# A windowed attention and MLP block on one core: a new order of the stages on every engine, PSUM banks dealt anew, and the first MLP layer in three f16 passes

## The chip, the core and the metric

The kernel runs on one core of one Trainium2 chip. A core has TensorE (PE, matmuls and their weight loads), VectorE (DVE), ScalarE (ACT), GpSimd (POOL) and SyncE (SP, which issues DMAs); each has its own queue of instructions, done in order, and they meet through semaphores. Engines read and write SBUF; matmuls write PSUM, which VectorE and ScalarE read. The metric is the device time of one execution in microseconds.

## What is computed

For 32 images of 96 channels and 56x56 pixels: layer norm over channels, attention with 12 heads of 8 channels inside windows of 7x7 pixels with a bias table, a projection and a residual sum, a 3x3 depthwise convolution with batch norm, and an MLP of 96 -> 384 -> 96 with a residual sum.

```python
xn = _layernorm(xw, ln_g, ln_b)
qkv = (xn @ qkv_w.T + qkv_b).reshape(Bw, N, 3, HEADS, HEAD_DIM)
...
attn = jnp.einsum('bhnd,bhmd->bhnm', q * SCALE, k)
attn = attn + bias.transpose(2, 0, 1)[None]
attn = jax.nn.softmax(attn, axis=-1)
out = jnp.einsum('bhnm,bhmd->bhnd', attn, v)
return out @ proj_w.T + proj_b
...
seq = shortcut + out
conv = lax.conv_general_dilated(x_local, conv_w, (1, 1), ((1, 1), (1, 1)), feature_group_count=DIM)
bn = (conv - bn_mean) * scale + bn_b
h = jax.nn.gelu(seq2 @ w1.T + b1, approximate=False)
seq = seq2 + (h @ w2.T + b2)
```

Inputs, weights and output are f32.

## The kernel before

A **chunk** is seven image rows, that is eight windows of 49 pixels or 392 columns (`CT`); there are 256 chunks, eight to an image. The program is a software pipeline: step n starts chunk n and carries older chunks further, and every engine's queue holds 264 steps, unrolled, with no branch in them. `real(st, lag)` drops what lies outside the 256 chunks. A chunk goes through these stages, with the step's lag in brackets.

- Layer norm (0): `centred` (TensorE, f32, into `d_ps`), the square (ScalarE), `variance` (TensorE, f32, into `a_ps`), logarithm and exponential for the reciprocal root (ScalarE), the product `xn` (VectorE), its f16 upper part `xh` (ScalarE) and lower part `xl` (GpSimd).
- Queries and keys (1): `three` f16 passes each, 392 columns, into `d_ps` and `b_ps`; each result is again split into an upper (ScalarE) and a lower part (VectorE), and SP sends six terms by DMA into `q_all` and `k_all` (`term`, counted by `exp_in`).
- Values (2): twelve f16 matmuls of 96 columns into `b_ps`, copied by ScalarE (`v32` for the even window of a pair) and VectorE (for the odd one).
- Maxima (2): four groups `max_scores` of 24 small matmuls (64 columns of weights, 49 moving) into `sm_ps`, each followed by VectorE's `maxima`; the row maxima are transposed on TensorE (`maxima_rows`), copied by VectorE (`mxt_out`) and sent by DMA into a row of `q_all`.
- Scores (3, the last group at 4): four groups `exp_scores` of 24 into `st_ps`, each followed by ScalarE's exp into `p32`; then four groups `values_times_p` of 12 f32 matmuls into `o_ps`, copied by ScalarE in halves (`outputs`) and sent by GpSimd's DMAs into `ox`.
- Sums' reciprocals (ScalarE) and `normalise` (VectorE), `projection` (TensorE, f32, four pieces, into `b_ps`), and the residual sum into `ximg` (VectorE, `sum_done`), all at 5.
- Convolution (6 and 7): the first tap on GpSimd, `tap` 1 to 8 on VectorE, each adding to `s2`.
- MLP (7 and 8): three `hidden` matmuls (f32, 96 to 128, one for each block of 128) into `a_ps`, `d_ps`, `b_ps`, a gelu each on ScalarE, three `second` matmuls (f32) into `a_ps`, the sum `y` on VectorE and the store. Gelu needs another activation table than exp and logarithm: two table loads a step.

Each engine's order is written out by hand in its `step`. `st_ps` and `sm_ps` have two PSUM banks each; `o_ps`, `a_ps`, `b_ps` and `d_ps` have one each and are shared by the stages above, so a stage also waits until the bank's last reader is done. On TensorE a step ends with `values_times_p(st, 3, 0)`, a wait for the fourth maximum, `values_times_p(st, 3, 1)`, `maxima_rows` and two `hidden`; the third stands at the start of the next step, followed by the first `max_scores`.

## Time and profile before

| | us |
|---|---|
| median of 3 runs | 3758.8 |
| lowest and highest run | 3752.88, 3760.82 |
| the profiled execution | 3757.64 |
| its span, from the first to the last instruction | 3755.8 |
| TensorE busy in the span | 3535.0 |
| ScalarE busy | 3101.7 |
| VectorE busy | 2937.8 |
| GpSimd busy | 1133.5 |

The granted clock of TensorE was 0.996 of full over the span. Busy times of TensorE include matmul ends that are modelled, so distances from one start to the next say more of its pace. Group rows give a count, the busy time and the mean of one; a bracket or a last column names what the engine waited for just before.

### The profile page before, as it was taken

What the parts mean: (1) busy time and instruction counts of PE and PEld (TensorE: products, weight loads), DVE (VectorE), ACT (ScalarE), POOL (GpSimd) and SP (SyncE); (2) the same over time, 40 slices, a digit from 0 to 9 for tenths busy, and PEclk for the clock granted to TensorE, in tenths of its full rate; (3) what the DMA queues carried; (4) which work ended last, traced back from release to release, by engine and by line L of the source; (5) the groups of instructions that cost most, each with busy time, mean ns of one, the idle gap of its engine ahead of it and who ended that gap; (6) DMA issues with size and microseconds to landing.
All of it is one profiled execution on the core that took longest, in us unless ns stands there. A gap on an engine that the chain in (4) does not pass through costs nothing.

```text
span 3755.8 us, 189287 instructions
## 1 busy us (share of the span) xinstructions
PE 3535.0 (94%) x83724; PEld 2303.3 (61%) x83724; DVE 2937.8 (78%) x5155; ACT 3101.7 (83%) x5123; POOL 1133.5 (30%) x1550
## 2 busy tenths in 40 slices
PE   4999999999999999999999999999999999999998
PEld 2666666666666666666666666666666666666664
DVE  4778787877878778787877878787787878778786
ACT  2788888888888888888888888888888888888886
POOL 2232332323233232333233233232323323232332
PEclk9999999999999999999999999999999999999999
DMA  1232332323233232322323233232323223232321
GB/s 46 82 91 85 89 89 84 91 84 91 85 88 90 84 91 84 91 87 87 88 86 91 85 90 90 84 91 84 91 85 89 88 85 92 83 91 84 90 89 47
DMA packets 269476, 321.37 MB, mean 86 GB/s; under 512 B 55124, under 2 KB 252181, under 8 KB 268663
## 3 DMA queue, kind: packets, MB, share of 16 engines
q1 hardware_dynamic: 235894, 232.12, 21.6%
q0 software_dynamic: 32768, 77.14, 6.2%
q8 instruction: 665, 10.90, 1.3%
q14 instruction: 149, 1.21, 0.1%
HBM read 39.35 MB, written 38.54 MB: 21 GB/s over the span
## 4 chain that ended last, share of the span: by engine, by line
PE 76%; ACT 12%; DVE 7%; issue 4%; SPq 1%; DMA 0%; POOL 0%; POOLq 0%; DVEq 0%; ACTq 0%
PE a_ps L438 13%; PE sm_ps L322 10%; PE o_ps L339 8%; PE a_ps L357 6%; PE a_ps L430 6%; DVE mx L673 5%; PE st_ps L307 5%; PE d_ps L349 5%; PE b_ps L430 4%; PE d_ps L430 4%; ACT sq L561 4%; PE b_ps L280 4%; ACT sq L563 4%; ACT sq L557 3%; PE b_ps L282 2%
## 5 line engine op out<-in xcount | busy, mean ns | idle before, releaser
L695 DVE SCALAR_TENSOR_TENSOR s<-ximg,cols,s 96x392 f32<-96x392 f32 x2048 | 1260.0, 615 | 20.8 <-POOL s L597 2.9
L673 DVE TENSOR_REDUCE mx<-sm_ps 128x12 f16<-128x588 f32 x1024 | 780.9, 763 | 435.4 <-PE sm_ps L322 435.4
L597 POOL TENSOR_TENSOR s<-ximg,cols 96x392 f32<-96x392 f32 x256 | 215.6, 842 | 2384.7 <-DVE y L726 2384.7
L499 ACT ACTIVATE p<-st_ps 128x588 f32<-128x588 f32 x1024 | 669.5, 654 | 130.7 <-PE st_ps L307 126.6
L322 PEld LDWEIGHTS sm_ps<-k_all,q_all 127*64 127x64 f16 x24576 | 472.5, 113 | 315.6 <-issue 210.5
L438 PE MATMUL a_ps<-g,w_s 128*96 128x392 f32 x1536 | 602.2, 501 | 0.0
L604 POOL DMA_DIRECT2D ox<-o_sb x1024 | 580.8, 570 | 47.9 <-issue 31.8
L322 PE MATMUL sm_ps<-k_all,q_all 127*64 127x49 f16 x24576 | 580.5, 192 | 7.9 <-DMA q_all<-ql 6.4
L307 PEld LDWEIGHTS st_ps<-q_all,k_all 128*64 128x64 f16 x24576 | 476.1, 113 | 151.8 <-issue 147.9
L307 PE MATMUL st_ps<-q_all,k_all 128*64 128x49 f16 x24576 | 562.3, 191 | 0.0
L339 PE MATMUL o_ps<-p,v 128*32 128x49 f32 x24576 | 428.1, 211 | 131.0 <-DVE mx L673 129.5
L339 PEld LDWEIGHTS o_ps<-p,v 128*32 128x32 f32 x24576 | 322.5, 110 | 324.6 <-DVE mx L673 164.6
L592 POOL TENSOR_TENSOR xl<-xn,xh 96x392 f16<-96x392 f32 x256 | 330.9, 1293 | 172.6 <-ACT xh L567 172.5
L542 ACT ACT_TABLE_LOAD x256 | 328.4, 1283 | 4.5
L536 ACT ACT_TABLE_LOAD x256 | 328.4, 1283 | 4.5
L737 DVE TENSOR_TENSOR xn<-d_ps,sq 96x392 f32<-96x392 f32 x256 | 143.8, 562 | 238.3 <-ACT sq L563 238.3
L438 PEld LDWEIGHTS a_ps<-g,w_s 128*96 128x96 f32 x1536 | 230.9, 164 | 105.2 <-issue 89.6
L567 ACT ACTIVATE xh<-xn 96x392 f16<-96x392 f32 x256 | 138.2, 540 | 160.8 <-DVE xn L737 160.8
L357 PE MATMUL a_ps<-sq,avg 96*96 96x392 f32 x512 | 233.0, 537 | 24.3 <-ACT sq L557 1.8
L557 ACT ACTIVATE sq<-d_ps 96x392 f32<-96x392 f32 x256 | 126.1, 492 | 151.3 <-PE d_ps L349 151.3
L519 ACT ACTIVATE o_sb<-o_ps 128x294 f32<-128x294 f32 x512 | 213.1, 416 | 43.3 <-PE o_ps L339 43.3
L430 PE MATMUL a_ps<-s,w_s 96*128 96x392 f32 x512 | 237.7, 546 | 6.9 <-DVE s L695 6.9
(98 smaller groups left out, 5539.7 us busy)
## 6 DMA issues: line engine op xcount, KB each, us to landing
ox<-o_sb POOLq DMA_DIRECT2D x1024, 73.5 KB, 2.6
k_all<-kh SPq DMA_DIRECT2D x512, 96.0 KB
q_all<-qh SPq DMA_DIRECT2D x512, 96.0 KB
x_sb<-in_x SPq DMA_DIRECT2D x256, 147.0 KB, 2.4
out<-y SPq DMA_DIRECT2D x256, 147.0 KB, 2.9
k_all<-kl SPq DMA_DIRECT2D x256, 96.0 KB
q_all<-ql SPq DMA_DIRECT2D x256, 96.0 KB
q_all<-mxt SPq DMA_DIRECT2D x256, 12.0 KB, 2.0
```

Of the source, the lines that this page charges most:

```text
L307: last = mm(st_ps[64 * w:64 * w + 64, h // HH, c0:c0 + TOK], k_all[:, r, h, n:n + WP], q_all[:, r, h, n:n + TOK], start=True, stop=True)
L322: last = mm(sm_ps[64 * w:64 * w + 64, h // HH, c0:c0 + TOK], q_all[0:MAXROW, r, h, n:n + WP], k_all[0:MAXROW, r, h, n:n + TOK], start=True ...
L339: last = mm(o_ps[32 * c4:32 * c4 + 32, at:at + TOK], v32[:, r, h, q, :], p32[:, q, h, :], start=True, stop=True)
L357: mm(a_ps[0:C, 0:CT], avg[:, :], sq[:, :], start=True, stop=True).then_inc(var_done, 1)
L430: mm(t[:, 0:CT], w1_s[:, k * 128:(k + 1) * 128], s2[0:C, (st[1] - lag) % 2, :], start=True, stop=True)\
L438: last = mm(a_ps[0:C, 0:CT], w2_s[:, k, :], g[:, k, :], start=k == 0, stop=k == NB - 1)
L499: af(p32[:, q, :, :].rearrange("p (b h) n -> p b h n", b=2), st_ps[:, :, 0:HALF].rearrange("p b (h n) -> p b h n", n=TOK), ACT.Exp).then_i ...
L536: af(g[:, k, :], (a_ps, d_ps, b_ps)[k][:, 0:CT], ACT.Gelu, bias=b1_c[:, k:k + 1]).then_inc(g_done, 1)
L592: tt(xl[0:C, r, :, 0:TOK], xn[:, :, :], xh[0:C, r, :, 0:TOK], ALU.subtract).then_inc(xl_done, 1)
L604: nc.gpsimd.dma_start(ox[:, r4, x4, :], o_sb[x4::4, r4, :, :]).then_inc(o_in[r4], 16)
L673: v.tensor_reduce(mx[:, (st[1] - lag) % 2, :, p].rearrange("p (b h) -> p b h", b=2), sm_ps[:, :, 0:HALF].rearrange("p b (h n) -> p b h n", ...
L695: v.scalar_tensor_tensor(acc, image_rows(st, lag, k // 3, k % 3), cw_c[:, k:k + 1], acc, ALU.mult, ALU.add)\
```

## The change

**Order and lags.** All engines get a new order of stages, and each stage names its chunk as `s - lag`; a wait counts chunks, with a semaphore for each of the four parts of a stage. The last `exp_scores` keeps its chunk but moves to the end of a step, and the first `max_scores` moves from lag 2 to lag 1 at the step's very end. `maxima_rows` stands behind the three `hidden`, and `mxt_out`'s copy is the first thing in VectorE's next step. VectorE takes the fourth maximum ahead of the normalisation, and taps 1 and 2 after the image sum. ScalarE does its three gelus between two table loads at the start of a step. SP issues three terms of one chunk, then an input load, the maxima row, and three terms of the next chunk with a store among them; the program has 266 steps.

**Banks.** `centred`, the third `hidden` and all `second` use `b_ps`; variance, queries, projection and one `hidden` use `a_ps`; keys, values and one `hidden` use `d_ps`. `free` waits for a bank's last real reader.

**First MLP layer.** Its input is split into f16 parts by two new GpSimd instructions (`image_high`, `image_low`), its weights, times 256, at setup; each of the three blocks is three f16 passes in place of one f32 matmul.

**Small changes.** Score matmuls load 49 columns of weights instead of 64, so they write 49 of 64 PSUM rows (the rest is set to zero once). The values are copied by one VectorE instruction, which writes two neighbouring words per value with a column of factors that is zero for the other window; ScalarE's copy goes. The setup has two instructions more for the weights, two for the zeros, one load, and the first input loads come behind it.

```diff
-STEPS = CHUNKS + 8
-IMAGE = C * SIDE * SIDE
+STEPS = CHUNKS + 10
...
+        w1_h, w1_l = sb("w1_h", [C, HID], F16), sb("w1_l", [C, HID], F16)
+        sh, sl = sb("sh", [C, CT], F16), sb("sl", [C, CT], F16)
...
+        def free(eng, *users):
+            for s, c in users:
+                if real(c):
+                    eng.wait_ge(s, c + 1)
+                    return
...
+            for s in range(STEPS):
+                term(q_all, 0, qh, qh_done, s - 3)
+                term(q_all, 2, ql, ql_done, s - 3)
+                term(k_all, 2, kh, kh_done, s - 3)
+                load(s)
+                maximum_row(s - 4)
+                first_term(q_all, 1, qh, qh_done, s - 2)
+                term(k_all, 1, kl, kl_done, s - 2)
+                store(s - 10)
+                term(k_all, 0, kh, kh_done, s - 2)
...
+                    free(pe, (mxt_out, c-1), (max_done[3], c-1), (max_done[2], c-1), (max_done[1], c-1), (max_done[0], c-1))
...
+                        last = mm(sm_ps[64 * w:64 * w + TOK, h // HH, c0:c0 + TOK], q_all[0:MAXROW, r, h, n:n + TOK],
                                   k_all[0:MAXROW, r, h, n:n + TOK], start=True, stop=True)
...
+            def hidden(c, k):
+                if not real(c):
+                    return
+                if k == 1:
+                    wait(pe, sl_done, c)
                 if k == 0:
-                    wait(pe, tap_done, st, lag, 8)
-                    if real(st, 0):
-                        wait(pe, lnv_done, st, 0)
-                    else:
-                        wait(pe, y_done, st, 8)
+                    free(pe, (sum_done, c+2), (lnv_done, c+7), (ql_done, c+6), (g_done[0], c-1))
                 elif k == 1:
-                    if real(st, 0):
-                        wait(pe, xn_done, st, 0)
-                    elif real(st, 1):
-                        wait(pe, ql_done, st, 1)
-                    else:
-                        wait(pe, g_done, st, 8, NB, 2)
-                elif real(st, 6):
-                    wait(pe, sum_done, st, 6)
-                t = (a_ps, d_ps, b_ps)[k]
-                mm(t[:, 0:CT], w1_s[:, k * 128:(k + 1) * 128], s2[0:C, (st[1] - lag) % 2, :], start=True, stop=True)\
-                    .then_inc(hid_done, 1)
...
+                    free(pe, (v32_done, c+5), (kl_done, c+6), (g_done[1], c-1))
+                elif k == 2:
+                    free(pe, (xn_done, c+7), (y_done, c-1), (g_done[2], c-1))
+                wide_three(hidden_ps[k][:, 0:CT], w1_h[:, k * 128:(k + 1) * 128], w1_l[:, k * 128:(k + 1) * 128], sh[:, :], sl[:, :]).then_inc(hid_done[k], 1)
+            def second(c, k):
+                if not real(c):
+                    return
+                wait(pe, g_done[k], c)
+                if k == 1:
+                    free(pe, (g_done[2], c+0), (xn_done, c+7), (y_done, c-1))
+                wide(b_ps[0:C, 0:CT], w2_s[:, k, :], g[:, k, :], start=k == 1, stop=k == 0).then_inc(s_done[k], 1)
...
+            for s in range(STEPS):
+                keys(s - 1)
...
+                max_scores(s - 1, 0)
...
+                af(g[:, k, :], {0: a_ps, 1: d_ps, 2: b_ps}[k][:, 0:CT], ACT.Gelu, bias=b1_c[:, k:k + 1], scale=1 / UP).then_inc(g_done[k], 1)
...
+            for s in range(STEPS):
+                act.preload_act_table_set("gelu_and_others")
+                gelu(s - 8, 1)
+                gelu(s - 8, 2)
+                gelu(s - 8, 0)
...
...
+                pool.sem_inc(turn, 1)
+                nc.gpsimd.tensor_copy(sh[:, :], s2[0:C, c % 2, :]).then_inc(sh_done, 1)
+            def image_low(c):
+                if not real(c):
+                    return
+                wait(pool, sh_done, c)
+                tt(sl[:, :], s2[0:C, c % 2, :], sh[:, :], ALU.subtract).then_inc(sl_done, 1)
+            for s in range(STEPS):
+                first_tap(s - 6)
+                to_channels(s - 4)
+                image_high(s - 7)
+                image_low(s - 7)
+                input_low(s)
...
+                wait(dve, v_done, c)
+                wait(dve, pv_done[2], c - 2)
+                v.tensor_tensor(v32[:, c % 2, :, :, :].rearrange("p h n (d x) -> p (h n d) x", x=4)[:, :, 0:2],
+                                d_ps[:, 0:NP * C].unsqueeze(2).broadcast_to([128, NP * C, 2]),
+                                half_c[:, :].unsqueeze(1).broadcast_to([128, NP * C, 2]), ALU.mult).then_inc(v32_done, 1)
...
+            for s in range(STEPS):
+                maxima_out(s - 3)
...
+                tap(s - 6, 2)
...
+    half = np.zeros((128, 2), np.float32)
+    for w in range(2):
+        half[64 * w:64 * w + TOK, w] = 1 / UP
```

On TensorE, from the wait for the fourth maximum to the next step's first maxima group (`o_ps` is the values' product, `sm_ps<-eye_h,mx` the transpose, `a_ps`, `d_ps`, `b_ps<-s,w_s` the first layer). Before:

```order
L339 MATMUL o_ps<-p,v 32x49 [waits p_done,max_done]
L339 MATMUL o_ps<-p,v 32x49 x11
L446 MATMUL sm_ps<-eye_h,mx 48x128
L430 MATMUL a_ps<-s,w_s 128x392 [waits lnv_done,tap_done]
L430 MATMUL d_ps<-s,w_s 128x392 [waits xn_done]
L430 MATMUL b_ps<-s,w_s 128x392 [waits sum_done]
L322 MATMUL sm_ps<-k_all,q_all 64x49 [waits max_done,mxt_out,exp_in1]
L322 MATMUL sm_ps<-k_all,q_all 64x49 x23
```

After, from the last block of the first layer on (`w_h`, `w_l` and `sh`, `sl` are the f16 parts; projection and the other two blocks stand in front of it):

```order
L256 MATMUL a_ps<-sh,w_h 128x392 [waits sum_done]
L257 MATMUL a_ps<-sl,w_h 128x392
L258 MATMUL a_ps<-sh,w_l 128x392
L319 MATMUL sm_ps<-eye_h,mx 48x128 [waits max_done3]
L289 MATMUL st_ps<-q_all,k_all 49x49 [waits p_done2]
L289 MATMUL st_ps<-q_all,k_all 49x49 x23
L310 MATMUL sm_ps<-k_all,q_all 49x49 [waits mxt_out,exp_in1]
L310 MATMUL sm_ps<-k_all,q_all 49x49 x23
```

The transpose with its wait went behind the first layer and behind both value groups, an exp group came between it and the maxima group, and that group, which waits for `mxt_out` and the DMA terms, is now of the chunk that was begun one step ago, directly ahead of the keys.

On VectorE, around the normalisation (`xn`), the image sum (`ximg`) and the first taps (`s<-ximg,cols,s`). Before:

```order
L737 TENSOR_TENSOR xn<-d_ps,sq 96x392 [waits xl_done,rstd_done]
L673 TENSOR_REDUCE mx<-sm_ps 128x12 [waits sm_done]
L695 SCALAR_TENSOR_TENSOR s<-ximg,cols,s 96x392 [waits tap0_done]
L746 SCALAR_TENSOR_TENSOR ximg<-b_ps,cols,x_sb 96x7x56 [waits proj_done]
L753 COPY mxt<-sm_ps 48x128 [waits row_in1,mxt_done]
L695 SCALAR_TENSOR_TENSOR s<-ximg,cols,s 96x392 [waits tap_done]
```

After:

```order
L771 TENSOR_TENSOR xn<-b_ps,sq 96x392 [waits xl_done,rstd_done]
L781 SCALAR_TENSOR_TENSOR ximg<-a_ps,cols,x_sb 96x7x56 [waits proj_done]
L725 SCALAR_TENSOR_TENSOR s<-ximg,cols,s 96x392 [waits tap_done0]
L725 SCALAR_TENSOR_TENSOR s<-ximg,cols,s 96x392 [waits tap_done1]
L709 COPY mxt<-sm_ps 48x128 [waits row_in0,mxt_done]
L725 SCALAR_TENSOR_TENSOR s<-ximg,cols,s 96x392 [waits tap_done2]
```

The fourth maximum moved ahead of the normalisation and is not in these rows any more; both taps of the younger chunk stand between the image sum and the copy of the maxima, on which TensorE's last group waits.

## Rows read from the trace of the kernel before

**Rows 1.** The page: busy time by engine (1), and the chain that ended last (4).

```profile
PE 3535.0 (94%) x83724; PEld 2303.3 (61%) x83724; DVE 2937.8 (78%) x5155; ACT 3101.7 (83%) x5123; POOL 1133.5 (30%) x1550
...
PE 76%; ACT 12%; DVE 7%; issue 4%; SPq 1%; DMA 0%; POOL 0%; POOLq 0%; DVEq 0%; ACTq 0%
```

**Rows 2.** Timeline: start us, duration, engine, line, operation, count. VectorE's output write, far apart.

```profile
502.53 0.62 DVE L726 SCALAR_TENSOR_TENSOR y<-a_ps,cols,s 96x392 f32<-96x392 f32 x1
...
3500.84 0.62 DVE L726 SCALAR_TENSOR_TENSOR y<-a_ps,cols,s 96x392 f32<-96x392 f32 x1
```

**Rows 3.** Waits: engine and line waited <- who: us in total, times, longest.

```profile
PEld o_ps L339 <- DVE mx L673: 164.6, 255, 1.4
...
PEld a_ps L357 <- ACT sq L557: 54.5, 255, 1.9
```

**Rows 4.** Timeline of one step, TensorE's matmuls (start, duration of a merged group).

```profile
2001.92 0.90 PE L357 MATMUL a_ps<-sq,avg 96*96 96x392 f32 x2
...
2004.36 0.47 PE L339 MATMUL o_ps<-p,v 128*32 128x49 f32 x24
...
2005.33 0.47 PE L339 MATMUL o_ps<-p,v 128*32 128x49 f32 x24 [0.50 <-DVE mx L673]
...
2005.90 0.93 PE L430 MATMUL a_ps<-s,w_s 96*128 96x392 f32 x2
...
2006.66 0.82 PE L430 MATMUL d_ps<-s,w_s 96*128 96x392 f32 x2
...
2008.07 0.56 PE L322 MATMUL sm_ps<-k_all,q_all 127*64 127x49 f16 x24
...
2008.47 0.54 PE L307 MATMUL st_ps<-q_all,k_all 128*64 128x49 f16 x24
...
2008.94 0.37 PE L280 MATMUL d_ps<-xh,wq_h 97*96 97x392 f16 x1
...
2009.15 0.33 PE L281 MATMUL d_ps<-xl,wq_h 97*96 97x392 f16 x1
...
2009.32 0.33 PE L282 MATMUL d_ps<-xh,wq_l 97*96 97x392 f16 x1
...
2012.04 0.73 PE L339 MATMUL o_ps<-p,v 128*32 128x49 f32 x48
...
2012.69 0.56 PE L322 MATMUL sm_ps<-k_all,q_all 127*64 127x49 f16 x24
```

**Rows 5.** Groups of instructions: count | busy us, mean ns of one | idle before.

```profile
L673 DVE TENSOR_REDUCE mx<-sm_ps 128x12 f16<-128x588 f32 x1024 | 780.9, 763 | 435.4 <-PE sm_ps L322 435.4
...
L438 PEld LDWEIGHTS a_ps<-g,w_s 128*96 128x96 f32 x1536 | 230.9, 164 | 105.2 <-issue 89.6 <-ACT g L536 0.8
...
L731 DVE TENSOR_SCALAR v<-b_ps 49x384 f32<-49x384 f32 x256 | 219.5, 857 | 9.2 <-PE b_ps L282 1.3
...
L430 PEld LDWEIGHTS d_ps<-s,w_s 96*128 96x128 f32 x512 | 97.6, 191 | 71.6 <-issue 0.6
```

**Rows 6.** Timeline of the same step, VectorE and GpSimd.

```profile
2005.19 0.61 DVE L695 SCALAR_TENSOR_TENSOR s<-ximg,cols,s 96x392 f32<-96x392 f32 x1
2005.26 1.31 POOL L592 TENSOR_TENSOR xl<-xn,xh 96x392 f16<-96x392 f32 x1 [0.41 <-ACT xh L567]
...
2005.73 0.62 DVE L746 SCALAR_TENSOR_TENSOR ximg<-b_ps,cols,x_sb 96x392 f32<-96x392 f32 x1
...
2006.27 0.21 DVE L753 COPY mxt<-sm_ps 48x128 f16<-48x128 f16 x1
...
2006.40 0.61 DVE L695 SCALAR_TENSOR_TENSOR s<-ximg,cols,s 96x392 f32<-96x392 f32 x1
```

**Rows 7.** Timeline, GpSimd, in the first steps, where no taps run yet.

```profile
68.86 0.90 POOL L592 TENSOR_TENSOR xl<-xn,xh 96x392 f16<-96x392 f32 x1 [11.54 <-ACT xh L567]
```

**Rows 8.** DMA issues: one from the step's timeline, one from the page (6).

```profile
2012.50 1.43 SPq L237 DMA_DIRECT2D k_all<-kh  x2
...
x_sb<-in_x SPq DMA_DIRECT2D x256, 147.0 KB, 2.4
```

710 lines of the change are left out of this document (345 added, 365 removed).

## The prediction

> **What bounds the kernel now.** First the page: TensorE holds 76% of the chain that ended last and is busy 94% of the span [rows 1]. Those matmul ends are modelled, so the timeline has to say how tight it is. The work repeats once per chunk of seven image rows: the same VectorE instruction stands at 502.53 and 3500.84 us, 210 steps apart, so one step takes 2998.31 / 210 = 14.28 us [rows 2]. 256 steps are 3656 us; the other 100 us of the 3755.8 us span are setup, filling and draining.
>
> Then one step of TensorE, by start-to-start distances [rows 4]. A group of 24 small score matmuls takes 0.40 us before another such group (2008.07 to 2008.47) and 0.47 before a whole-array matmul (to 2008.94). One f16 pass of 392 columns takes 0.17 (2009.15 to 2009.32). A 392-column f32 matmul, two instructions, takes about 0.66, but 0.76 when what stands before it is not f32 (2005.90 to 2006.66). Two value groups take 0.65 (2012.04 to 2012.69). In another place the first value group alone fills 0.97 us (2004.36 to 2005.33), where it should need 0.33: TensorE's second group waits there for VectorE's fourth maximum, 164.6 us in all, 0.64 per step [rows 3]. The variance matmul waits 54.5 / 256 = 0.21 for the square [rows 3]. So 14.28 - 0.64 - 0.21 = 13.4 us of a step are TensorE's own queue, and 0.85 are waits. VectorE and ScalarE are busy 2937.8 / 256 = 11.5 and 3101.7 / 256 = 12.1 us per step [rows 1]. TensorE bounds, with one VectorE chain on top.
>
> **The change, part by part.** (1) First MLP layer in f16. Its three f32 matmuls take 2008.07 - 2005.90 = 2.17 us [rows 4]. Nine f16 passes of 0.17 take 1.53: -0.64.
>
> (2) The order on TensorE. Queries now follow an f32 matmul rather than small groups, -0.13 at the rates above. Three groups lose an edge, -0.09. More f32 matmuls stand alone, after small or f16 work (+0.10 each by 0.76 against 0.66) or in front of small groups (+0.09 each, as 2008.07 - 2005.90 - 0.76 - 0.66 = 0.75 shows for the third of three): I count three and a half such edges more, +0.33. Net +0.1. TensorE's queue: 13.4 - 0.64 + 0.1 = 12.9 us.
>
> (3) Score matmuls load 49 columns of weights instead of 64. Twelve pairs in 0.40 us, 0.02 of it start-up, are 32 ns per pair. The moving side, 49 columns at the 0.42 ns each that 0.17 us for 392 gives, is 20 ns, so it does not fill the pair. The weight side does: 96 against 128 f32 columns load in 164 and 191 ns [rows 5], 27 ns for 32 columns in two halves, so 0.42 ns per column and 27 ns for 64 f16 columns. 49 columns would need 21, saving 6 ns x 12 pairs x 8 groups = 0.6 us. The bounds are nothing (if the 32 ns is a price of issuing) and 0.6. I take 0.6, since 27 + 5 fits 32 and the value groups issue twice as many matmuls per round without being slower per instruction. TensorE: 12.3 us.
>
> (4) The waits. Laid end to end in the new order with these distances, and counted from the keys' first pass, centred starts at 5.1 us, variance at 6.9, projection at 9.1, hidden 1 at 9.9, the transpose at 11.4 and the last group, the next chunk's first maxima, at 11.9. Offsets below are in this layout; those of the other engines follow from it by the durations of the rows. The transpose of the maxima now stands behind the whole first layer, so VectorE's fourth maximum, due about 9.1 us into the step, is not waited for until 11.4: the 0.64 goes. The square has exp scores and values in front of variance now, so the 0.21 goes too. Next late is a new loop at the end of the step. The first maxima group of the next chunk waits for `mxt_out`, the copy of the previous maxima, and VectorE gives that only after projection -> image sum -> tap 1 -> tap 2. From the start of projection TensorE needs 0.81 + 1.53 + 0.15 + 0.33 = 2.8 us to reach that group. The loop needs 0.97 for projection's data, 0.05 of handoff, 0.54 image sum (2005.73 to 2006.27), 0.65 tap 1 (0.61 and a handoff to the tap that reads it), 0.53 tap 2 (2005.19 to 2005.73 is such a distance), 0.21 copy, 0.05 = 3.0 [rows 6]. That is +0.2: 12.5 us per step. Behind the waiting group stands all of the next step's TensorE work.
>
> (5) GpSimd in the way of the taps. GpSimd's `xl` takes 0.90 us alone [rows 7] but 1.31 in every steady step [rows 6]: it starts 0.07 us after a tap, and the missing 0.41 is about the rest of that tap. So a tap, which reads two SBUF tensors, and a GpSimd elementwise instruction do not run together. No row shows the other order, a tap that meets a running `xl`; its cost is between nothing and the whole 0.90. Variance to `xl` takes 2005.26 - 2001.92 = 3.34 us [rows 4, 6]. Now variance starts 2.18 before projection (0.80 + 0.33 + 0.30 + 0.75), and VectorE reaches the normalisation 0.1 later behind the fourth maximum, so `xl` starts 1.25 after projection and tap 1 is due at 0.97 + 0.05 + 0.54 = 1.56. `xl` comes first by 0.3 and reads until about 2.05 to 2.15. I take a full hold, 0.45 to 0.5, because the exclusion seen one way is nearly complete. The step: 12.5 + 0.45 = 12.95 us.
>
> The Trainium skill, "SBUF — State Buffer", section "SBUF: two separate sides", states this as an exclusive lock of one port pair: a VectorE instruction with two SBUF inputs and a GpSimd instruction that reads SBUF hold it for the whole instruction, and whoever comes second waits. It speaks against this change, which puts two more elementwise instructions on GpSimd. By it the hold is full (12.95); without it the step is 12.5.
>
> (6) The rest. The two GpSimd instructions that split the image into f16 parts (my estimate 0.6 to 0.9 and 0.9, from `xl` alone) start after tap 8, about 7.7 us into the step, and end at 9.4. Hidden 1 wants them at 9.9: hidden, with 0.5 to spare. No tap is due in that time. ScalarE loses the 0.86 copy of the values (about 11.3 us busy left), and its gelus end about 0.8 before their users. SP issues as many DMAs as before at 0.72 each [rows 8]. But the first maxima group of a chunk has moved up by more than half a step: six terms and a store go out from `qh_done` (4.7), the last at 8.9, landing by 11.3 if they take 2.4 us as an input load does [rows 8]. It is wanted at 12.5: hidden, with about 1 us to spare, and every us beyond that costs 1 us per step. Setup and two more steps at the ends: 100 becomes 105 us.
>
> The values copy on VectorE writes 768 elements in pairs instead of 384 single ones. The single ones take 857 ns, a 588-element maximum 763 [rows 5]. At the latter's rate (588 elements, about 0.15 fixed) 768 take 0.95 us; at the former's 1.56. I take 0.95, as VectorE's other instructions go at that rate; the slow case moves the normalisation 0.5 later, which lets tap 1 pass `xl` or sets `xl` between the taps: 12.6 to 13.3 us. The Trainium skill, "Vector Engine (DVE) Microarchitecture Reference", section "Measured stream behaviour on trn2", says that single hops cost extra and pairs of adjacent words on 8-byte boundaries do not, which agrees with the 857 ns and would give the 0.95.
>
> **Sum.** 256 x 12.95 = 3315; + 105 = 3420 of span; + 2 for what lay around the profiled span (3757.64 against 3755.8); the median lay 1 us above the profiled run. Forecast 3422 us, -9%.
>
> **Rivals.** (A) The taps are not held by a running `xl`. For it: the tap at 2006.40 started 0.17 before `xl` ended and took its usual 0.61 [rows 6]. Against it: reads may end before the instruction does. 12.5 x 256 + 107 = 3307 us. (B) The narrower weights bring nothing. For it: pairs of 32 ns could be an issue price. Against: the arithmetic of (3). Projection comes 0.45 later and `xl` 0.3, so the hold shrinks to 0.35: 13.35 x 256 + 107 = 3525; without any hold 13.0, 3435. (C) Slower: all four GpSimd elementwise instructions get in front of a tap, and VectorE becomes the bound. Its own queue is 11.2 to 11.8 us; four holds of 0.85 make it 14.6 to 15.2, as VectorE may not overlap them: 14.6 x 256 + 107 = 3845. It decides against the change from 14.28 - 12.5 = 1.8 us of hold per step on the loop of (4). Against it: only `xl` and the first tap's own instruction meet two-input VectorE work by my layout. (D) Something with little margin comes late: the DMA terms (1 us to spare), the f16 split (0.5) or the gelus (0.8). Each us past its margin is a us per step; at 13.6 to 14.0 us, 3590 to 3690. That the change does not do what it says leaves nothing to gain from: the order of instructions is fixed in the program.
>
> **How the numbers follow.** Forecast 0.45, A 0.20, B with hold 0.14 and without 0.06, D 0.10, C 0.05. The range, 3290 to 3570, holds the forecast, A, both of B, and the slow values copy. A measurement of this kernel can tell about 0.2% from no change. Faster 0.94, same 0.01, slower 0.05.
>
> **What would show it.** The step in the profile after: 12.95 us. The score groups at 0.33 us before another (0.40 would be B). The three first-layer matmuls within 1.53. Tap 1 starting right when `xl` ends, or stretched past 0.61 (the hold), or neither (A). TensorE's wait in front of the first maxima group, about 0.2 to 0.65 per step, ended by VectorE's copy; a DMA there would be D. The values copy at 0.95. What would make me wrong most: a wait inside TensorE's queue that I have laid out as just met (sums of many distances of 0.05 to 0.1 us).

## The result and the profile after

The changed kernel takes 3619.5 us (median of 4 runs, 3601.3 to 3629.8) against 3756.7 for the kernel before (4 runs, 3752.9 to 3760.8). The ratio is 0.9629, with a 95% interval of 0.9589 to 0.9670: 3.7% faster, where 9% was forecast. The time lies above the range, and inside what rival D gave (3590 to 3690 us).

The page of the kernel after: busy time by engine (1), and the chain that ended last by engine and by line (4).

```profile
PE 3288.9 (91%) x84492; PEld 2151.8 (59%) x84492; DVE 3151.9 (87%) x5159; ACT 2902.8 (80%) x4887; POOL 1427.1 (39%) x2062
...
PE 27%; DMA 17%; DVE 15%; ACT 14%; SPq 14%; issue 11%; POOL 1%; ACTq 0%; POOLq 0%; DVEq 0%
DMA k_all<-kh 17%; SPq L211 12%; PE b_ps L252 11%; PE sm_ps L310 5%; DVE s L725 4%; ACT g L514 3%; DVE ox L716 2%; ACT L551 2%; DVE mx L699 2%; PE d_ps L256 2%; SPq L230 2%; ACT p L463 2%; DVE y L762 2%; DVE v L752 2%; PE a_ps L252 2%
```

Before, TensorE held 76% of that chain [rows 1]. Now it holds 27%, and SyncE's issuing and the DMAs together hold 31%: another resource has taken over.

The second look is at the steps. From one write of `y` to the next, the kernel before took 14.27 us, within 0.1 us in 244 of its first 246 steps. The kernel after has a floor of 12.99 us, and it is on it (within 0.1) in 96 of 246; 42 steps are over 1 us longer, up to 18.4. Above the floor lie 172 us in all, 0.7 per step. So the step that the prediction laid out (12.95) is there; what it did not have is that most steps miss it, by amounts that look like chance.

What TensorE waits for, in the kernel after (us in total, times, longest):

```profile
PE sm_ps L310 <- DMA k_all<-kh: 197.9, 184, 4.3
PE d_ps L256 <- POOL sl L621: 36.9, 13, 4.5
PE sm_ps L310 <- DVE mxt L709: 31.0, 63, 0.5
```

The first maxima group waits 184 times for a DMA, and 63 times for the copy that the prediction expected there. The chain of waits around one of the long steps, in order of time (start us, length, what):

```profile
2711.91 0.40 ACT qh L505
...
2712.39 0.70 SPq L211
...
2716.53 6.10 DMA k_all<-kh
...
2722.67 0.76 PE sm_ps L310 x12
...
2727.79 0.51 ACT qh L505
```

This is a closed loop: the query's high part, six terms, the landing of the last, the first maxima group, and 5.1 us later the next query. In an undisturbed step those 5.1 us are 4.1. What lengthens them is in the same stretch of TensorE's timeline and in its windows (columns: stretch, its length, busy time and instructions of TensorE, its weight loads, VectorE, ScalarE and GpSimd, the granted clock, DMA share, GB/s):

```profile
2722.67 0.76 PE L310 MATMUL sm_ps<-k_all,q_all 127*49 127x49 f16 x24 [2.47 <-DMA k_all<-kh]
```

```profile
2717.00:2719.00 2.00, 2.00 (x47) 1.47 (x35) 1.57 (x4) 1.82 (x4) 1.16 (x2) 1.00 0.62 176
...
2723.00:2725.00 2.00, 2.00 (x24) 1.31 (x19) 1.49 (x3) 0.56 (x2) 0.00 (x0) 0.50 0.00 0
```

After 2.47 us of waiting TensorE goes on at a granted clock of 0.50, the lower of its two levels (1.2 GHz), although it is fully busy then. Summed over windows of 2 us, from 150 us to the end of the 246 steps, busy time lost to the lower clock (busy time times the missing share of the clock) is 60 us in the kernel after and 0 in the kernel before. So a long wait is paid for twice. SyncE and GpSimd in the same stretch:

```profile
2713.86 0.46 SPq L230 DMA_DIRECT2D out<-y  x1
...
2716.53 0.67 SPq L211 DMA_DIRECT2D k_all<-kh  x1
2717.25 0.68 SPq L205 DMA_DIRECT2D x_sb<-in_x  x1
...
2713.82 2.27 POOL L605 DMA_DIRECT2D ox<-o_sb  x4 [0.18 <-issue]
```

GpSimd issues its four transfers of `ox` from 2713.82 to 2716.09, between SyncE's second and last terms (issued at 2713.13 and 2716.53). The page's median landing of the input load, which goes out right behind the last term, has gone from 2.4 us [rows 8] to 4.0:

```profile
x_sb<-in_x SPq DMA_DIRECT2D x256, 147.0 KB, 4.0
```

Worked out from the trace for all chunks, the last of the six terms lands 4.4 us (median) after its issue, from 3.5 (5th percentile) to 5.4 (90th) and 6.5 at most. In the kernel before it was 2.8, from 2.6 to 4.1.

### The profile page after: what moved, and what is told of

It is laid out like the page before. It is cut to its first block, busy times and chain, and to the rows that moved or that the text cites. A ratio compares the mean times of both kernels' runs of the same rounds, so it can differ in the third digit from the quotient of the medians.

```text
span 3618.7 us, 192106 instructions
## 1 busy us (share of the span) xinstructions
PE 3288.9 (91%) x84492; PEld 2151.8 (59%) x84492; DVE 3151.9 (87%) x5159; ACT 2902.8 (80%) x4887; POOL 1427.1 (39%) x2062
## 4 chain that ended last, share of the span: by engine, by line
PE 27%; DMA 17%; DVE 15%; ACT 14%; SPq 14%; issue 11%; POOL 1%; ACTq 0%; POOLq 0%; DVEq 0%
DMA k_all<-kh 17%; SPq L211 12%; PE b_ps L252 11%; PE sm_ps L310 5%; DVE s L725 4%; ACT g L514 3%; DVE ox L716 2%; ACT L551 2%; DVE mx L699 2%; PE d_ps L256 2%; SPq L230 2%; ACT p L463 2%; DVE y L762 2%; DVE v L752 2%; PE a_ps L252 2%
## 5 line engine op out<-in xcount | busy, mean ns | idle before, releaser
L310 PEld LDWEIGHTS sm_ps<-k_all,q_all 127*49 127x49 f16 x24576 | 421.2, 105 | 567.1 <-DVE mx L699 280.6
L310 PE MATMUL sm_ps<-k_all,q_all 127*49 127x49 f16 x24576 | 521.5, 188 | 229.8 <-DMA k_all<-kh 197.9
L252 PE MATMUL b_ps<-g,w_s 128*96 128x392 f32 x1536 | 677.7, 525 | 0.0
L289 PE MATMUL st_ps<-q_all,k_all 128*49 128x49 f16 x24576 | 524.9, 187 | 2.6 <-ACT p L463 2.6
L289 PEld LDWEIGHTS st_ps<-q_all,k_all 128*49 128x49 f16 x24576 | 422.6, 104 | 170.0 <-ACT p L463 149.4
L781 DVE SCALAR_TENSOR_TENSOR ximg<-a_ps,cols,x_sb 96x392 f32<-96x392 f32 x256 | 159.4, 623 | 127.4 <-PE a_ps L252 127.4
L252 PEld LDWEIGHTS b_ps<-g,w_s 128*96 128x96 f32 x1536 | 238.8, 169 | 49.6 <-issue 8.8
L716 DVE TENSOR_TENSOR ox<-ox,inv 96x392 f32<-96x392 f32 x256 | 257.6, 1006 | 1.1 <-ACT inv L479 1.1
L252 PE MATMUL b_ps<-x_sb,center 96*96 96x392 f32 x512 | 233.4, 538 | 23.0 <-DMA x_sb<-in_x 23.0
L621 POOL TENSOR_TENSOR sl<-s,sh 96x392 f16<-96x392 f32 x256 | 240.5, 939 | 21.7
```

The costliest lines, as they stand in the source:

```text
L252: return mm(o, w, m, start=start, stop=stop)
L289: last = mm(st_ps[64 * w:64 * w + TOK, h // HH, c0:c0 + TOK], k_all[:, r, h, n:n + TOK], q_all[:, r, h, n:n + TOK], start=True, stop=True)
L310: last = mm(sm_ps[64 * w:64 * w + TOK, h // HH, c0:c0 + TOK], q_all[0:MAXROW, r, h, n:n + TOK], k_all[0:MAXROW, r, h, n:n + TOK], start=Tr ...
L716: v.tensor_tensor(ox[:, c % 2, 0:2, :], ox[:, c % 2, 0:2, :], inv[:, :, :], ALU.mult).then_inc(norm_done, 1)
```

## What the runs were to tell apart

The theory: the terms are issued too late for what a DMA takes at that place, where `ox` lies in their middle. Two forms of it differ: a lack of margin (any landing time would do if the terms went out earlier) and the coincidence itself. Rivals: another wait is the cause and the DMA only appears last; traffic of chance, such as the loading of instructions, delays the terms; or the sum's own terms (weights, hold, loop) are wrong and happen to add up. The first runs undo one part of the DMA order each, the later ones undo one term of the sum. All edits are of the changed kernel unless said otherwise; e3_both_late serves as a quieter base for the terms.

### Moving `ox` and the store

GpSimd's order in e1_ox_late:

```diff
                 first_tap(s - 6)
-                to_channels(s - 4)
                 image_high(s - 7)
                 image_low(s - 7)
                 input_low(s)
+                to_channels(s - 4)
```

> The changed kernel, with GpSimd's four transfers into `ox` moved behind `xl`, so that they leave SP's six terms alone. In the changed kernel the last of the six terms lands 4.4 us (median) after its issue, about when the first maxima group wants it, and each late one stops TensorE: steps of 13.0 us with many of 13.5 to 18 among them. Theory 1 (the two sets of transfers share the DMA engines, and that makes the terms late): the last term lands in about 3 us, as it does before the change, the waits of the maxima group for a DMA (253 us in the trace) fall below 60, and the time falls by 130 to 190 us, to 3430 to 3490. Theory 2 (SP issues the terms too late, and what else moves does not matter): landing 4 us or more, time within 20 us of 3620. Theory 3 (instruction fetches or other traffic of chance delay them): the same as theory 2. Against all: ScalarE's logarithm of the sums may now wait for `ox` (wanted about 2.2 us after the last of these transfers is issued), which would cost up to 0.5 us per step, 130 us.

Measured: 3526.8 us, ratio 0.9386 (0.9368 to 0.9404).

SyncE's order in e2_store_late:

```diff
                 load(s)
+                store(s - 10)
                 maximum_row(s - 4)
                 first_term(q_all, 1, qh, qh_done, s - 2)
                 term(k_all, 1, kl, kl_done, s - 2)
-                store(s - 10)
                 term(k_all, 0, kh, kh_done, s - 2)
```

> The changed kernel, with the output store moved out from among the six terms and put behind the input load. The last three terms are issued 0.5 us earlier, and 147 KB less compete with them. Theory 2 (the issue is late): waits for DMAs fall by about 0.5 us in each late step (perhaps two steps in three), 60 to 120 us faster than 3620. Theory 1 (the transfers into `ox` are what delays): 0.5 us of margin is gained all the same, but landing stays above 4 us: 30 to 90 us faster. Theory 3: long delays of chance stay (steps of 15 to 18 us), 20 to 60 us faster.

Measured: 3599.3 us, ratio 0.9580 (0.9553 to 0.9606). The gain of 20 us is barely clear of the scatter: this interval and that of the changed kernel overlap.

e3_both_late has both edits.

> Both moves together. Theory 1: no wait for a DMA is left in the maxima group, and every step takes the 13.0 us that undisturbed steps take: 256 x 13.0 + 105 = 3433 us, between 3420 and 3450, unless the logarithm of the sums waits for `ox`. Theory 2: as with the store alone, 3500 to 3560. Theory 3: long steps remain, above 3520.

Measured: 3488.6 us, ratio 0.9291 (0.9277 to 0.9305). It stays some 40 us short of what was expected, and its waits say why, TensorE's first, then ScalarE's (in total, times, longest):

```profile
PE sm_ps L310 <- DVE mxt L709: 129.2, 229, 2.0
PE sm_ps L310 <- DMA k_all<-kh: 28.5, 24, 3.9
...
ACT inv L472 <- DMA ox<-o_sb: 69.1, 71, 4.0
```

The terms are no longer late, and the copy is the usual wait again, as forecast. But `ox` itself, issued until 9.6 us into the step, now lands at about the time when ScalarE wants it: the edit traded one late DMA for another. The longest of these waits, 4.0 us, and seven more stand behind pauses of GpSimd that the next section but one shows.

### The first maxima group later

e4_max0_later moves the consumer instead: the first maxima group of a chunk goes behind the keys and `second`, which gives the terms about a microsecond more.

```diff
-                max_scores(s - 2, 1)
+                max_scores(s - 2, 0)
                 second(s - 8, 2)
                 queries(s - 1)
+                max_scores(s - 2, 1)
...
                 exp_scores(s - 3, 3)
-                max_scores(s - 1, 0)
```

> The changed kernel, with the first maxima group put 1.3 us further on: behind the keys and one matmul of the second layer in the next step, and the second group behind the queries. The DMAs are untouched, so landing stays at 4.4 us, but the group wants them 1.3 us later and waits no longer for the copy of the maxima either. All DMA theories: waits for DMAs fall by more than half, since most late steps are late by under 1.3 us. If VectorE has room for its first two maxima later, the gain is 100 to 180 us and steps could even fall to 12.6 to 12.8 (no wait for the copy): 3400 to 3520. If the second maximum then holds up the tap, keys' lower part and image sum behind it on VectorE (which is busy 12.2 of 13.0 us), steps grow to 13.5 or more and the time stays within 50 us of 3620.

Measured: 3686.3 us, ratio 0.9813 (0.9797 to 0.9830). The waits of its TensorE:

```profile
PE d_ps L256 <- ACT g L514: 166.6, 239, 0.7
PE b_ps L252 <- DVE y L762: 88.2, 248, 0.4
...
PE sm_ps L310 <- DMA k_all<-kh: 8.4, 15, 1.5
```

The wait for the DMA falls from 198 to 8 us and 221 of 246 steps are alike, so margin does cure the unevenness; the landing time is still 4.5 us. But the floor is 13.80, because TensorE now waits for ScalarE and VectorE, and the cure costs more than the illness.

### Terms that go out as soon as they can

h1_keys_first leaves `ox` where the change put it and orders the six terms by when their sources are written: three of them do not need the query.

```diff
-                term(q_all, 0, qh, qh_done, s - 3)
-                term(q_all, 2, ql, ql_done, s - 3)
-                term(k_all, 2, kh, kh_done, s - 3)
                 load(s)
+                store(s - 10)
                 maximum_row(s - 4)
-                first_term(q_all, 1, qh, qh_done, s - 2)
+                first_term(k_all, 0, kh, kh_done, s - 2)
+                term(k_all, 2, kh, kh_done, s - 2)
                 term(k_all, 1, kl, kl_done, s - 2)
-                store(s - 10)
-                term(k_all, 0, kh, kh_done, s - 2)
+                term(q_all, 1, qh, qh_done, s - 2)
+                term(q_all, 0, qh, qh_done, s - 2)
+                term(q_all, 2, ql, ql_done, s - 2)
```

> Edit: the changed kernel with nothing moved but SyncE's loop: the six terms go out as both high parts of the keys, low part of the keys, then the three of the queries, instead of queries first and the keys' high part last, and the store of the output goes behind the load (as in e2_store_late, which alone measured 3599). GpSimd issues `ox` where the change put it. The keys' high part is written 1.6 us before the queries' and their low part at the step's end, so three terms go out before the queries are there and only three afterwards: the last is issued about 1.8 us into the step instead of 4.4. Theory (the lateness is lack of margin: terms issued at 4.4 land after 4.4 us, at 8.8, when they are wanted at 8.6): even a landing of 4.4 to 5.4 now ends at 6.2 to 7.2, the step is 13.0 nearly everywhere, 3435 to 3465 us, with `ox` still in the middle. Rival (what delays the terms is a backlog of the engines that `ox` makes, however early they are issued, or the lateness of `ox` itself makes ScalarE wait): 3490 to 3600.

Measured: 3482.3 us, ratio 0.9268 (0.9253 to 0.9284). 211 of 246 steps are on the floor of 12.98, although a term still lands 4.5 us after its issue (median). It misses its range by 17 us, and what is left is in eight steps of 16.8 to 18.5 us, 37 us in all. TensorE's wait there, and GpSimd in one of them:

```profile
PE d_ps L256 <- POOL sl L621: 37.4, 12, 4.5
```

```profile
1319.12 0.83 POOL L593 TENSOR_TENSOR s<-ximg,cols 96x392 f32<-96x392 f32 x1 [6.40 <-DVE y L762]
1323.18 2.27 POOL L605 DMA_DIRECT2D ox<-o_sb  x4 [3.23 <-issue]
1325.46 0.65 POOL L614 CAST sh<-s 96x392 f16<-96x392 f32 x1
1326.19 1.12 POOL L621 TENSOR_TENSOR sl<-s,sh 96x392 f16<-96x392 f32 x1
```

GpSimd stands still for over 3 us in front of its transfers although nothing that the profile shows holds it. From the end of its last wait for a semaphore to the first of the four issues it takes 3.56 us, where 0.56 is usual. It does this eight times, once in 31 chunks, and so it does, at the same eight chunks, in the kernel before, the kernel after and every variant whose `ox` GpSimd issues. The two instructions that split the image stand behind it in its queue, and the first layer waits for them: 2.8 us of waiting each time, 22.7 in all (the other 14.7 of the 37.4 come while the pipeline drains), and the clock that falls after such a wait makes up the rest of the 37.

h4_e3_keys_first is h1_keys_first with `ox` issued behind `xl`.

> Edit: e3_both_late with the order of terms of h1_keys_first. Differs from h1_keys_first only in where GpSimd issues `ox` (behind `xl`, until 9.6 us into the step, instead of 1.8 to 4.1). Theory: the terms are early in both, so what differs is whether `ox` lands in time; here it lands near 11.8 and ScalarE wants it at 11.3 to 11.8 (it waited 69 us in e3_both_late): 3455 to 3480, not faster than h1_keys_first. Rival (transfers of `ox` amid the terms cost even when the terms have margin): h1_keys_first is slower than this one by 20 us or more.

Measured: 3471.1 us, ratio 0.9245 (0.9231 to 0.9259). It is 11 us faster than h1_keys_first (the intervals overlap), where over 20 would have spoken for the coincidence as such and none was expected. What differs is where the pauses of GpSimd come out. TensorE no longer waits for `sl` (13 us, all of them while the pipeline drains), but ScalarE waits 73 us for `ox`, 20 of them right behind the eight pauses; the steps around these lose about 19 us, with two of 17.1 and 18.1 us, where h1_keys_first loses 37.

### `ox` on SyncE's queue

f3_sp_ox removes the four transfers from GpSimd.

```diff
+            def to_channels(c):
+                wait(sp, proj_done, c - 2)
+                wait(sp, o_done[0], c)
+                wait(sp, o_done[1], c)
+                for x4 in range(4):
+                    sp.dma_start(ox[:, c % 2, x4, :], o_sb[x4::4, c % 2, :, :]).then_inc(o_in[c % 2], 16)
...
                 load(s)
+                store(s - 10)
+                to_channels(s - 5)
                 maximum_row(s - 4)
```

> Edit: from the changed kernel, SyncE stores the output behind the load instead of among the terms (as in e2_store_late), and the four transfers of `ox` are issued by SyncE right behind that store instead of by GpSimd; GpSimd keeps only its elementwise work. Theory (the late terms and, in e3_both_late, the late `ox` are DMA transfers that share the 16 engines at the wrong moment): in e3_both_late the terms land after 3.3 us, but `ox` is issued until 9.6 us into the step and ScalarE waits for it 69 us in all, once 4.0. SyncE is free from 5.7 us on, so `ox` goes out between 5.7 and 8.5 and lands before 11.2: step 13.0 nearly everywhere, 3433 to 3455 us. Rival (the queue that GpSimd feeds was not to blame, SyncE's own four transfers delay the row of maxima, issued at 8.6, and the terms): 3490 or more, with waits for the row before the first exp scores.

Measured: 5484.7 us, ratio 1.457. The loop index was one chunk too early. SyncE's largest wait, and TensorE behind it:

```profile
SPq L141 <- ACT o_sb L499: 3258.7, 256, 14.5
```

```profile
2007.74 0.76 PE L300 MATMUL st_ps<-q_all,k_all 128*49 128x49 f16 x24 [5.25 <-DMA q_all<-mxt]
2008.99 1.62 PE L263 MATMUL b_ps<-x_sb,center 96*96 96x392 f32 x2
```

SyncE waited for outputs that ScalarE had not yet written, and the row of maxima and all six terms of the next chunk stood behind it. f4_sp_ox_copy is the same with the copy of the maxima moved; it repeats the mistake and tells only that.

> Edit: f3_sp_ox, and on VectorE the copy of the maxima `mxt_out` stands between tap 1 and tap 2 instead of behind tap 2. Theory (a step of 13.0 is TensorE's own queue of 12.45 plus 0.55 of waiting for that copy at the end of the loop projection, image sum, tap 1, tap 2, copy): the copy comes 0.54 earlier, TensorE's wait of 0.55 in front of the first maxima group goes, and the step is 12.45 to 12.6: 3290 to 3340 us. Rival (what bounds the 13.0 step is another loop, for instance VectorE's own queue of 12.3 us busy per step or ScalarE's): the wait moves elsewhere and the step stays at 12.9 to 13.0, 3410 to 3450.

Measured: 5389.9 us, ratio 1.433. With `to_channels(s - 6)` it becomes g1_sp_ox:

> Edit: as f3_sp_ox, but SyncE issues `ox` one chunk later in its own loop (chunk s-6 instead of s-5). In f3_sp_ox SyncE asked for a chunk whose last outputs ScalarE had not yet written: it waited up to 14.5 us per chunk for them, and the row of maxima and all six terms of the next chunk stood behind that wait. With s-6 the outputs have been written 4 us before SyncE comes to them. Theory (transfers at the wrong moment make the long steps): step 13.0 nearly everywhere, ScalarE's wait for `ox` and TensorE's for the terms both nearly gone: 3433 to 3460 us. Rival (a queue of SyncE's with eleven transfers per chunk is late by itself, or the transfers of `ox` in it delay the row of maxima): 3490 or more, and the wait before the exp scores names the row.

Measured: 3457.0 us, ratio 0.9204 (0.9190 to 0.9218). Floor 12.99, 203 of 246 steps on it, 18 us above it in all. Its waits (TensorE, ScalarE):

```profile
PE sm_ps L321 <- DVE mxt L719: 117.5, 223, 2.4
PE sm_ps L321 <- DMA k_all<-kh: 32.0, 30, 4.1
...
ACT inv L483 <- DMA ox<-o_sb: 18.9, 29, 1.4
```

This is the forecast's kernel as nearly as it was reached: 13.06 us per step against 12.95, and no pause of GpSimd.

### The terms of the sum, one by one

f5_base_no_xl is e3_both_late without `xl`; the low parts of the normalised input are left out.

```diff
-                tt(xl[0:C, c % 2, :, 0:TOK], xn[:, :, :], xh[0:C, c % 2, :, 0:TOK], ALU.subtract).then_inc(xl_done, 1)
+                pool.sem_inc(xl_done, 1)
```

> Edit: e3_both_late without GpSimd's subtraction `xl` (its semaphore is raised at once, the low parts of the normalised input are left out). It takes away what the prediction said holds tap 1. Theory of the hold (term 5): tap 1 falls from 1.01 to 0.61 us, the copy comes 0.4 earlier, TensorE's wait falls from 0.55 to 0.15 and the step from 13.0 to 12.6, so 3488 - 100 = 3385 us; less if `ox`, which GpSimd issues 0.9 earlier now, no longer makes ScalarE wait. Rival A (tap 1 is long for another reason, such as its reading `ximg` right behind the write): tap 1 stays at 1.0 and the step at 13.0.

Measured: 3420.7 us, ratio 0.9099 (0.9085 to 0.9113). The timeline of e3_both_late, then of f5_base_no_xl, at the same place of a step (image sum, taps 1 and 2 merged, copy, first maxima group):

```profile
1109.68 0.62 DVE L781 SCALAR_TENSOR_TENSOR ximg<-a_ps,cols,x_sb 96x392 f32<-96x392 f32 x1 [0.43 <-PE a_ps L252]
1110.22 1.66 DVE L725 SCALAR_TENSOR_TENSOR s<-ximg,cols,s 96x392 f32<-96x392 f32 x2
1111.81 0.21 DVE L709 COPY mxt<-sm_ps 48x128 f16<-48x128 f16 x1
...
1109.91 0.91 POOL L585 TENSOR_TENSOR xl<-xn,xh 96x392 f16<-96x392 f32 x1 [0.96 <-ACT xh L544]
...
1112.16 0.50 PE L310 MATMUL sm_ps<-k_all,q_all 127*49 127x49 f16 x24 [0.54 <-DVE mxt L709]
```

```profile
1095.24 1.27 DVE L725 SCALAR_TENSOR_TENSOR s<-ximg,cols,s 96x392 f32<-96x392 f32 x2
1096.43 0.21 DVE L709 COPY mxt<-sm_ps 48x128 f16<-48x128 f16 x1
...
1096.79 0.50 PE L310 MATMUL sm_ps<-k_all,q_all 127*49 127x49 f16 x24 [0.15 <-DVE mxt L709]
```

Two taps take 1.66 us beside `xl` and 1.27 without it, TensorE's wait falls from 0.54 to 0.15, and the floor from 13.00 to 12.60. The 0.39 passes one to one into the step. The time misses the expected 3385 because the uneven steps are back (81 us): a step that is 0.4 shorter has 0.4 less margin for the terms, and TensorE's waits for them in these steps grow from 21 to 51 us.

f1_base_64 is e3_both_late with 64 columns of weights again.

```diff
-                        last = mm(st_ps[64 * w:64 * w + TOK, h // HH, c0:c0 + TOK], k_all[:, r, h, n:n + TOK],
+                        last = mm(st_ps[64 * w:64 * w + 64, h // HH, c0:c0 + TOK], k_all[:, r, h, n:n + WP],
```

> Edit: e3_both_late with 64 columns of weights again in both kinds of score matmul (zero columns behind the 49, as in the kernel before). It undoes term (3) of the prediction alone. That term was 0.6 us per step: eight groups of 0.40 instead of 0.33. Theory: one of the eight groups lies between projection and the first maxima group, where TensorE waits anyway, so 7 x 0.07 = 0.5 us per step come back: step 13.5, 3488 + 125 = 3615 us. Rival (rival B: the pairs have a price of issuing, the columns cost nothing; the 0.34 us of the changed kernel comes from the new order of groups): no change, 3485 to 3500.

Measured: 3523.9 us, ratio 0.9376 (0.9360 to 0.9391). Its groups:

```profile
1131.44 0.56 PE L310 MATMUL sm_ps<-k_all,q_all 127*64 127x49 f16 x24
1131.84 0.54 PE L289 MATMUL st_ps<-q_all,k_all 128*64 128x49 f16 x24
...
1136.34 0.56 PE L310 MATMUL sm_ps<-k_all,q_all 127*64 127x49 f16 x24 [0.43 <-DVE mxt L709]
```

A group takes 0.40 us, where the narrow ones take 0.34 (1112.16 stands for them; two neighbours in the kernel after start at 1131.68 and 1132.03). The columns cost what was forecast, and rival B falls. But the floor rises only from 13.00 to 13.21, not by 0.5: projection comes later relative to `xl`, tap 1 takes 0.81 instead of 1.01 us, and the wait for the copy shrinks from 129 to 73 us.

e5_before_49 makes the same edit alone in the kernel before, the other way (49 instead of 64).

> Edit: the kernel before with 49 instead of 64 columns of weights in both kinds of score matmul (the rows of PSUM that are no longer written are set to zero once). It does term (3) of the prediction alone. Theory (about 0.42 ns per weight column): groups of 0.34 instead of 0.40 us, eight of them, less what lies behind TensorE's two waits: step 13.75 to 13.9 instead of 14.28, ratio 0.963 to 0.975, 3620 to 3665 us. Rival B (a price of issuing, 32 ns per pair): same as before, 3757.

Measured: 3711.3 us, ratio 0.9882 (0.9868 to 0.9897). Two waits of its TensorE, and two groups:

```profile
PE o_ps L339 <- DVE mx L675: 120.5, 255, 1.4
PE a_ps L357 <- DVE y L728: 78.5, 247, 0.3
```

```profile
2008.44 0.50 PE L322 MATMUL sm_ps<-k_all,q_all 127*49 127x49 f16 x24
2008.78 0.48 PE L307 MATMUL st_ps<-q_all,k_all 128*49 128x49 f16 x24
```

The groups are 0.34 us there too, 0.06 x 8 = 0.48 us shorter per step, but the step goes from 14.27 to 14.11: 78.5 / 256 = 0.31 us per step is now a wait in front of variance, for VectorE's `y`, which reads that bank; before, only its weight load waited there, for the square, 0.21 [rows 3]. The expectation took off too little for it.

f2_base_f32 is e3_both_late with the first layer in f32 and without GpSimd's two splitting instructions.

```diff
-                wide_three(hidden_ps[k][:, 0:CT], w1_h[:, k * 128:(k + 1) * 128], w1_l[:, k * 128:(k + 1) * 128], sh[:, :], sl[:, :]).then_inc(hid_done[k], 1)
+                wide(hidden_ps[k][:, 0:CT], w1_s[:, k * 128:(k + 1) * 128], s2[0:C, c % 2, :]).then_inc(hid_done[k], 1)
```

> Edit: e3_both_late with the first MLP layer in f32 again, as in the kernel before (three f32 matmuls of the image sum with taps, and neither of GpSimd's two instructions that split it). It undoes term (1) of the prediction alone, -0.64 us per step in TensorE's queue. Theory: these matmuls lie between projection and the first maxima group, where TensorE waits 0.55 us for VectorE's copy; the 0.64 uses up that wait and the step grows by some 0.1 to 0.2 only (the transpose, 0.64 later, just precedes the copy): 13.1 to 13.2, 3510 to 3540 us. Rival (the term counts in full, as in the sum of the prediction): 13.65, 3650 us.

Measured: 3480.7 us, ratio 0.9265 (0.9251 to 0.9278), 8 us less than its base. TensorE around the layer:

```profile
1137.10 0.82 PE L252 MATMUL d_ps<-s,w_s 96*128 96x392 f32 x2
...
1139.17 0.24 PE L319 MATMUL sm_ps<-eye_h,mx 128*48 128x128 f16 x1
...
1139.80 0.50 PE L310 MATMUL sm_ps<-k_all,q_all 127*49 127x49 f16 x24
```

From its first pass to the transpose the layer takes 2.07 us instead of 1.59, the transpose ends just ahead of the copy, and the floor is 13.02 against 13.00. TensorE, which stood idle in front of the first maxima group, works instead: its wait for the copy falls from 129 to 13 us. The whole of term (1) is worth nothing in this kernel. In the kernels of the next section, where this wait is gone, it was not tested.

### The loop through the copy

g2_sp_ox_copy is g1_sp_ox with one line of VectorE moved:

```diff
             for s in range(STEPS):
-                maxima_out(s - 3)
                 tap(s - 7, 3)
...
                 tap(s - 6, 1)
+                maxima_out(s - 2)
                 tap(s - 6, 2)
```

> Edit: g1_sp_ox, and on VectorE the copy of the maxima stands between tap 1 and tap 2. f5_base_no_xl has shown that the loop projection, image sum, tap 1, tap 2, copy sets the step (12.6 instead of 13.0 us when tap 1 is 0.4 shorter). Theory: with the copy 0.54 earlier, tap 1 may be held as long as before, and TensorE's queue, 12.45 us, is what is left: step 12.5 to 12.6, 3300 to 3345 us, if `ox` is no longer late. Rival (the next loop is as long: terms of the query, DMA, first maxima group, or ScalarE's logarithms behind `ox`): 12.9 or more, 3410 or more.

Measured: 3423.1 us, ratio 0.9112 (0.9097 to 0.9127). Floor 12.58, as expected, but only 100 of 246 steps are on it, and 90 us lie above it. h2_all adds the order of terms of h1_keys_first.

> Edit: g2_sp_ox_copy with the order of terms of h1_keys_first. In g2_sp_ox_copy undisturbed steps take 12.6 us but many take 12.8 to 14; TensorE waits 58 us in all for the term that is issued last, 4.5 us into the step, and lands 3.3 later. Theory (margin again): the last term is issued at about 2.2, that wait goes, and so does most of the rest: steps of 12.5 to 12.6, 3310 to 3345 us, faster than every kernel so far. Rival (in g2_sp_ox_copy ScalarE's own queue, whose gelus and logarithms follow each other without a gap, sets the uneven steps): 3380 or more, with TensorE waiting for ScalarE.

Measured: 3393.7 us, ratio 0.9043 (0.9028 to 0.9057), the fastest version found, 6.2% under the changed kernel. 171 steps are on 12.58, TensorE's wait for the terms is gone, and it still misses 3345. Two rows of one of its long steps:

```profile
1331.43 0.39 PE L300 MATMUL st_ps<-q_all,k_all 128*49 128x49 f16 x15 [0.83 <-issue]
...
1336.21 0.74 PE L263 MATMUL a_ps<-ox,wp 96*96 96x196 f32 x3 [1.32 <-issue]
```

TensorE stops inside a group of 24, after the ninth matmul, and inside projection, and no semaphore ends the stop. Such stops add up to 49 us here, to 26 in g2_sp_ox_copy and to 6 in the kernel after. h3_keys_first_copy was to tell whether SyncE's issue of `ox` brings them: it is h1_keys_first with the same line moved.

> Edit: h1_keys_first, and on VectorE the copy of the maxima stands between tap 1 and tap 2. GpSimd still issues `ox` where the change put it. Theory (margin for the terms, then the loop of projection, image sum, taps and copy, then eight pauses of 3.56 us that GpSimd makes in front of its transfers, once in 31 chunks): the 0.39 to 0.54 us of the loop go from each of 256 steps as they did in f5_base_no_xl, and the pauses cost what they cost in h1_keys_first (some 40 us in all): 12.6 x 256 + 105 + 45 = 3375 us, 3365 to 3395. Rival (in g2_sp_ox_copy and h2_all the uneven steps came from a step of 12.6 as such, ScalarE being without a gap, not from SyncE's issue of `ox`): as uneven as h2_all and the pauses on top, 3420 or more.

Measured: 3479.2 us, ratio 0.9274 (0.9242 to 0.9306). The rival was right about the size: floor 12.58, but 131 us above it, 66 us of stops without a releaser, the eight pauses on top. So the stops do not depend on who issues `ox`. ScalarE was named as their cause; that it is not, since in h2_all it waits for TensorE in those steps. Nor does the length of the step alone bring them: f5_base_no_xl has 12.60 and 7 us of stops. What the three kernels with many stops share is that TensorE waits for nearly nothing in a step on the floor: 0.08 us, against 0.15 in f5_base_no_xl and 0.54 in the kernel after.

The traces point to the loading of TensorE's instructions. The page of h2_all has a DMA queue of this kind:

```profile
q8 instruction: 672, 11.01, 1.4%
```

These are 672 transfers of 16384 bytes, one for about 250 of TensorE's matmuls and weight loads. Each of the 39, 63 and 81 stops of over 0.25 us in g2_sp_ox_copy, h2_all and h3_keys_first_copy ends 1.1 to 1.7 us after such a transfer has ended; of TensorE's instructions in general, less than a fifth start in that stretch. No run changed the loading, so this stays an inference, if a strong one.

## Why the prediction was wrong

The runs side by side. The landing is that of the last term after its issue, median, worked out from the trace; "above" is the sum over 246 steps of what each takes beyond the floor.

| kernel | `ox` issued | landing us | floor us | above us | time us |
|---|---|---|---|---|---|
| before | right after the terms | 2.8 | 14.27 | 2 | 3756.7 |
| after | amid the terms | 4.4 | 12.99 | 172 | 3619.5 |
| e2_store_late | amid | 4.8 | 12.99 | 145 | 3599.3 |
| e1_ox_late | after `xl` | 3.2 | 13.00 | 72 | 3526.8 |
| e3_both_late | after `xl` | 3.3 | 13.00 | 41 | 3488.6 |
| e4_max0_later | amid | 4.5 | 13.80 | 49 | 3686.3 |
| h1_keys_first | amid, terms early | 4.5 | 12.98 | 47 | 3482.3 |
| h4_e3_keys_first | after `xl`, terms early | 3.3 | 12.99 | 36 | 3471.1 |
| g1_sp_ox | by SyncE, after the store | 3.3 | 12.99 | 18 | 3457.0 |

**The step that failed** is in part (6): the last term "landing by 11.3 if they take 2.4 us as an input load does", so "hidden, with about 1 us to spare". The layout around it was right: the budget between issue and need was 12.5 - 8.9 = 3.6, or 4.05 us with the hold that the next sum adds, and on the floor steps of e1_ox_late, which has the same order of terms, it is 4.2. The 2.4 was wrong. Its row [rows 8] is of an input load that SyncE issued in a quiet stretch, beside the small row of maxima alone; the kernel before had its own terms landing in 2.8, up to 4.1 in one of ten, and the change moves GpSimd's transfers between them. At 4.4 us the margin is below zero in the median. By the prediction's own rule that alone would make 3422 + (4.4 - 4.05) x 256 = 3512 us, 90 more than forecast. The trace has nearly that: within the 246 steps TensorE waits 80 us more in front of the maxima groups than it would on the floor. That the rule comes so close is in part luck, since with the measured margin of 4.2 it gives 51, and landings scatter, so that a late one costs what an early one does not give back. The other 108 us are things that the rule leaves out: the lower clock after long waits (60), waits behind GpSimd's pauses (below, 22), the two ends of the program (121 us in place of 105) and the floor (12.99 in place of 12.95, 10 us).

**How much of it is which.** On the changed kernel, the store out of the terms brings some 20 us, the order of the terms another 117 (e2_store_late to h1_keys_first, `ox` still amid them and the landing as long as before). Moving `ox` alone brings 93, but only 11 once the terms are early (both counts with what each gives back of the clock). So the two forms of the theory are one: the coincidence makes the landing long, and it costs only where there is no margin. The lack of margin is shown to be the cause: more margin at an unchanged landing (h1_keys_first) cures it, and so, for the most part, does a shorter landing (e1_ox_late).

**A part that no term had** is GpSimd's pause in front of its transfers. It costs 37 us in h1_keys_first. In the kernel after, eight of the thirteen waits for `sl`, 22 of the 36.9 us, stand behind it; the other 15 us come in the last 70 us, while the pipeline drains. The prediction gave the split of the image "0.5 to spare" and asked of GpSimd's queue only how long its instructions take. The pause was to be seen in the kernel before, where nothing stood behind it that anyone waited for. It is as long there, 3.55 us from the end of the last wait (546.14) to the issue; the first tap covers its beginning, so that 2.75 show as idle:

```profile
546.11 0.84 POOL L597 TENSOR_TENSOR s<-ximg,cols 96x392 f32<-96x392 f32 x1 [9.49 <-DVE y L726]
549.69 2.27 POOL L604 DMA_DIRECT2D ox<-o_sb  x4 [2.75 <-issue]
```

**What was right, by its steps.** (1) Nine f16 passes take 1.50 us (1.53). As a difference the layer gives 0.48 us (2.07 against 1.59 up to the transpose) in place of 0.64, and as a gain nothing: f2_base_f32 shows that it lies under the loop of (4), so that the 0.48 us of TensorE's work go into a wait. The prediction's own figures say so: with 2.8 + 0.6 us, TensorE would just have filled the 3.0 + 0.45 of the loop. A sum of a queue, followed by a loop on top, hides which terms count. (3) Groups at 0.34 us (0.33), in both kernels; worth 0.21 at the end of the changed kernel and 0.16 in the kernel before, not 0.6, for the same reason. Rival B had part of this: it let the hold shrink when projection comes later. (4) The two waits are gone, and the new one in front of the first maxima group is 0.15 without the hold (0.2) and about 0.55 with it (0.2 + 0.45). (5) Tap 1 takes 1.00 instead of 0.61 us behind a running `xl`, 0.39 where 0.45 to 0.5 were taken, and it goes one to one into the step (f5_base_no_xl): rival A falls. What spoke for A, a tap that started 0.18 before `xl` ended and was not held, fits too: a tap that starts 0.58 ahead of `xl`'s end takes 0.39 more, one that starts 0.39 ahead (f1_base_64) 0.20 more, so only the last 0.19 us of `xl` are free. The rule cited there, an exclusive lock of the port pair (the Trainium skill, "SBUF — State Buffer", "SBUF: two separate sides"), agrees with it in this order too, but for these 0.19 us. (2) was not tested by itself. The values copy takes 0.94 (0.95). The floor, 12.99 against 12.95, is thus right within 10 us over 256 steps, but in part because errors cancel: TensorE's queue is 12.45 us (12.99 less 0.54 of waiting) where 12.3 were laid out, the hold 0.39 for 0.45 and the wait 0.15 for 0.2. Of the miss of 198 us, 172 lie above the floor.

**Why the landing is longer** is argued, not shown. In the kernel after, SyncE's queue completes about 45 packets per half microsecond while `ox` is under way and about 70 otherwise, which is the pace at which it issues (96 packets in 0.67 us). GpSimd's packets are 4704 bytes each, those of a term 1024. So a backlog grows while `ox` is issued; over 2.3 us it comes to about 120 packets, 0.9 us at 70 per half microsecond (an estimate from these numbers), close to the 1.1 between the landings of e3_both_late (3.3) and of the kernel after (4.4). The Trainium skill, "DMA: Bandwidth & Descriptors", "Queues, rings and completion order", states that an engine with work in several queues takes turns between them and drains a whole packet, by which it means a group of descriptors, before it changes. That the queues share the engines agrees; what such a group holds in this kernel no run here shows. Why the landing does not return to 2.8 when `ox` is moved, but to 3.3, is open.

A part of the scatter goes with the loading of instructions, which the expectation of e1_ox_late named as a rival. In the kernel before, 141 of 245 last terms meet a transfer of the instruction queue between issue and landing, and 26 of them take over 4 us; of the 104 that meet none, 2 do. In the kernel after nearly every term meets one.

## What to carry to other kernels

Before a change pulls a consumer forward, write down for each DMA in its loop the time from issue to need, and compare it with the landing of that DMA among its new neighbours, at its ninth decile, not with a lone transfer's median. Order a queue's transfers by when their sources are ready; three of six terms did not have to wait for the query, and that order alone was worth 117 us. Look also for rare events that nothing in the old kernel waits for, such as a pause once in 31 chunks, before you put work behind them. And check each saving against the loop that sets the step: work taken from an engine inside a loop that another engine bounds turns into a wait.

## What the runs showed of the hardware

- GpSimd pauses in front of its DMA issues once in 31 chunks (124 transfers of `ox`), eight times in a run, at chunks 32, 63, 94 and so on to 249. From the end of its last wait to the issue it takes 3.54 to 3.57 us in all 13 kernels whose `ox` GpSimd issues, the kernel before among them. Nothing in the trace ends the pause.
- A lower clock follows a single wait. In the kernel after, 28 of the 29 stretches at 0.50 within the 246 steps begin within 6 us of a wait of TensorE of 1.5 to 3.0 us. Busy time lost to it, by windows of 2 us without the two ends of the program: 60 us in the kernel after, 46 in e2_store_late, 15 in e1_ox_late, 19 in h1_keys_first, 6 in e3_both_late, 0 in g1_sp_ox and in the kernel before. In f3_sp_ox, where a wait of 5.25 us comes in every step, the granted clock is 0.50 from 2008 to 2018 us with TensorE fully busy, and the f32 pair `center` that takes 0.90 us in the kernel after takes 1.62 (its profiled run had a mean granted clock of 0.753, the other three 0.776 to 0.780).
- Where TensorE's queue has nearly no wait left (0.08 us in a step of 12.58), it stops in the midst of a group with no releaser: 26, 49 and 66 us in all in g2_sp_ox_copy, h2_all and h3_keys_first_copy, against 7 in f5_base_no_xl, 6 in the kernel after and 1 before. Every stop of over 0.25 us ends 1.1 to 1.7 us after the end of a 16384-byte transfer of the instruction queue q8.
- The exclusion of a two-input VectorE instruction and a GpSimd one holds both ways: `xl` takes 1.31 us behind a tap [rows 6], a tap 1.00 behind `xl`, and `normalise` 1.02 beside GpSimd's first tap (0.56 before, where the two do not meet).
